# Ternary feed-forward stage: the convolution's middle tap from PE to DVE, the product with the token scales from DVE to GpSimd

## The reference, cut to what matters

```python
def act_quant(x):
    scale = 127.0 / jnp.clip(jnp.max(jnp.abs(x), axis=-1, keepdims=True), 1e-05)
    return jnp.clip(jnp.round(x * scale), -128, 127) / scale
def weight_quant(w):
    scale = 1.0 / jnp.clip(jnp.mean(jnp.abs(w)), 1e-05)
    return jnp.clip(jnp.round(w * scale), -1, 1) / scale
...
h = bit_linear(x, w1)                     # 256 -> 1024, both sides quantised
h = depthwise_conv1d(h.transpose(0, 2, 1), conv_w, conv_b)   # 3 taps along the tokens
h = jax.nn.silu(h.transpose(0, 2, 1))
return bit_linear(h, w2)                  # 1024 -> 256
```

## Time and profile before

| what | value |
|---|---|
| three timed runs | 4100.06, 4102.44, 4113.78 us (median 4102.44) |
| profiled execution | 4103.83 us, of which 4102.1 us is the span of the program |
| busy in the whole span | PE 3478.7 us (85%), DVE 2519.5 us (61%), ACT 1758.5 us (43%), POOL 1149.7 us (28%) |
| the changed stage | from about 736 to 1038 us of the span |
| POOL in this stage, 720 to 1040 us | 12.40 us busy |

### The profile page before, as it was taken

How to read it: one execution, slowest core, us unless ns; L and a number is a source line. 1 busy time by engine, 2 the same in 40 slices (tenths; PEclk the granted TensorE clock), 3 DMA queues, 4 the chain that set the end, 5 groups by cost and what they waited for, 6 DMA issues and landing times. The chain is left out here.

```text
span 4102.1 us, 68551 instructions
## 1 busy us (share of the span) xinstructions
PE 3478.7 (85%) x18821; PEld 1736.5 (42%) x18821; DVE 2519.5 (61%) x7412; ACT 1758.5 (43%) x2506; POOL 1149.7 (28%) x1242
## 2 busy tenths in 40 slices
PE   5999999799599999996997887887379999995797
PEld 2343343344233333334663555555223334335565
DVE  4666665677587777775215666677856666644531
ACT  1554545444044444452114666666525545550111
POOL 3343431000644444411113332231232221101132
PEclk8999999999699999997998989999679999995898
DMA  5322330000433223201008888898031122103142
GB/s 138 80 61 66 81 73 17 21 1 1 112 89 96 81 78 86 75 22 48 0 15 251 282 262 265 283 302 286 2 96 38 38 53 58 32 1 114 53 107 67
DMA packets 212161, 393.08 MB, mean 96 GB/s; under 512 B 24633, under 2 KB 76985, under 8 KB 211657
## 3 DMA queue, kind: packets, MB, share of 16 engines
q1 hardware_dynamic: 168777, 296.38, 26.2%
q10 hardware_dynamic: 36864, 83.90, 5.4%
q0 software_dynamic: 6144, 8.39, 1.2%
HBM read 189.88 MB, written 96.47 MB: 70 GB/s over the span
## 5 line engine op out<-in xcount | busy, mean ns | idle before, releaser
L428 DVE CUSTOM_DVE_ANT_0 A_sums<-A_p_ps,A_bias 128x512 bf16<-128x512 f32 x1536 | 1007.0, 687 | 418.1 <-PE A_p_ps L274 396.2
L501 ACT ACTIVATE A_probs<-A_p_ps 128x1024 f32<-128x1024 f32 x640 | 654.4, 1024 | 608.2 <-PE A_p_ps L293 595.9
L274 PE MATMUL A_p_ps<-A_k_stack,A_q_stack 96*128 96x512 bf16 x1536 | 514.2, 391 | 101.5 <-DVE A_nmax L428 91.5
L288 PE MATMUL A_p_ps<-A_q_stack,A_k_stack 99*128 99x512 bf16 x1536 | 461.3, 381 | 0.1
L303 PE MATMUL A_oT_ps<-A_probs,A_v_aug 128*17 128x512 f32 x3072 | 406.0, 600 | 3.2 <-ACT A_probs L501 2.4
L274 PEld LDWEIGHTS A_p_ps<-A_k_stack,A_q_stack 96*128 96x128 bf16 x1536 | 135.8, 98 | 485.4 <-DVE A_nmax L428 383.8
L293 PE MATMUL A_p_ps<-A_biasT,ident_bf 128*128 128x512 bf16 x1024 | 306.9, 380 | 0.0
L1000 PE MATMUL A_t_ps<-ident,A_scores 128*128 128x128 f32 x1280 | 206.8, 296 | 113.3 <-DVE A_probsT L1082 99.6
L1092 DVE CUSTOM_DVE_ANT_0 A_scores<-A_qk_ps,A_rel_in 128x384 f32<-128x384 f32 (+3 forms) x512 | 231.6, 485 | 78.7 <-PE A_qk_ps L977 76.0
L1082 DVE COPY A_probsT<-A_t_ps 128x1024 f32<-128x1024 f32 (+3 forms) x256 | 210.5, 822 | 107.8 <-PE A_t_ps L1000 100.0
L501 ACT ACTIVATE A_probs<-A_probs 128x1024 f32<-128x1024 f32 x128 | 135.3, 1057 | 312.7 <-DVE A_probs L443 312.7
(11 more groups left out here) (356 smaller groups left out, 5829.8 us busy)
## 6 DMA issues: line engine op xcount, KB each, us to landing
A_k_stack<-A_parts SPq DMA_DIRECT2D x192, 256.0 KB, 5.3
A_q_stack<-A_parts SPq DMA_DIRECT2D x192, 256.0 KB, 5.5
A_rel_dram<-A_rel_out ACTq DMA_DIRECT2D x64, 512.0 KB, 5.0
A_rel_in<-A_rel_dram SPq DMA_DIRECT2D x64, 512.0 KB
A_rel_dram<-A_rel_out ACTq DMA_DIRECT2D x64, 384.0 KB, 4.3
A_rel_in<-A_rel_dram SPq DMA_DIRECT2D x64, 384.0 KB, 4.8
A_ctxT<-in_ctxT SPq DMA_DIRECT2D x32, 512.0 KB, 6.2
A_mask_in<-in_mask SPq DMA_DIRECT2D x64, 256.0 KB, 4.1
```

The lines of the kernel that those rows point to most:

```text
L274: nc.tensor.matmul(p1_ps[i % 2][:, :], q_stack[0:KS, a_par, j * GH + i, t * P:(t + 1) * P], k_stack[0:KS, a_par, j * GH + i, :], start=Tru ...
L288: last = nc.tensor.matmul(p2_ps[half][:, i % 2, :], k_stack[:, par, j * GH + i, kb * P:(kb + 1) * P], q_stack[:, par, j * GH + i, :], star ...
L428: nc.vector.tensor_tensor_reduce(out=sums[:, i % NX, :], in0=p1_ps[i % 2][:, :], in1=bias[:, t, :], scale=-1.0, scalar=3.4028235e38, op0=A ...
L501: nc.scalar.activation(dst, src, ACT.Exp).then_inc(exp_done, 1)
```

## The change

- `tap_diag` keeps two blocks a unit (taps 0 and 2), and ACT builds 16 of them, not 24. `convolve` issues two fp32 matmuls, on `hs` shifted by 0 and by 2.
- The middle tap is a new DVE instruction, `add_centre`: `hs` times the tap (one scalar for each partition) plus `cv_ps`, written to a new SBUF tile `act_in` (`summed`). It waits for the unit's convolution and stands behind `round_unit` and ahead of `fold`. `silu` waits for `summed` and reads `act_in`. `cv_ps` and `hs` come free with `summed`.
- `quantise` moves from DVE to POOL and keeps its order by slots. On POOL, `inv_std(b+1)` stands in slot 1 ahead of that slot's `quantise`. `round_unit` stays on DVE and waits for POOL's product.

```diff
-        tap_diag = sb("tap_diag", [P, HC, 3, P], F32)
+        tap_diag = sb("tap_diag", [P, HC, 2, P], F32)
+        act_in = sb("act_in", [P, 2, S], F32)
...
+            def quantise(b, par, c):
+                if c == 0:
+                    pool.wait_ge(sc_ready, b + 1).then_inc(apart_pool, 1)
+                nc.gpsimd.tensor_tensor(act_out[:, par, c, :], act_out[:, par, c, :], sc_bc[:, par, :], ALU.mult).then_inc(u_done, 1)
+
+            def frame(b, par, slots):
+                for c in slots:
+                    if c == 1 and exists(b + 1) and exists(b):
+                        inv_std(b + 1)
+                    bq, pq, cq = quantised(b, par, c, LAG)
+                    if exists(bq):
+                        quantise(bq, pq, cq)
+
+            inv_std(0)
+            frames(pool, frame)
...
-                    pe.wait_ge(silu_done, unit(b, c) - 1)
-                for k in range(3):
-                    last = nc.tensor.matmul(cv_ps[c % 2][:, :], tap_diag[:, c, k, :], hs[:, c % 2, k:k + S],
-                                            start=k == 0, stop=k == 2)
+                    pe.wait_ge(summed, unit(b, c) - 1)
+                for k in range(2):
+                    last = nc.tensor.matmul(cv_ps[c % 2][:, :], tap_diag[:, c, k, :], hs[:, c % 2, 2 * k:2 * k + S],
+                                            start=k == 0, stop=k == 1)
...
-                    dve.wait_ge(conv_done, unit(b, c) - 1)
+                    dve.wait_ge(summed, unit(b, c) - 1)
...
+            def add_centre(b, c):
+                dve.wait_ge(conv_done, unit(b, c) + 1).then_inc(apart_dve, 1)
+                if not isinstance(b, int) or unit(b, c) >= 2:
+                    dve.wait_ge(silu_done, unit(b, c) - 1)
+                nc.vector.scalar_tensor_tensor(act_in[:, c % 2, :], hs[:, c % 2, 1:S + 1], taps[:, c, 1:2],
+                                               cv_ps[c % 2][:, :], op0=ALU.mult, op1=ALU.add).then_inc(summed, 1)
...
-                    if exists(bq):
-                        quantise(bq, pq, cq)
                     if exists(after[0]) and (c == HC - 1 or exists(b)):
                         scale(*after)
                     if exists(bq):
                         round_unit(bq, pq, cq)
+                    if exists(b):
+                        add_centre(b, c)
...
-                act.wait_ge(conv_done, unit(b, c) + 1).then_inc(apart_act, 1)
-                nc.scalar.activation(act_out[:, par, c, :], cv_ps[c % 2][:, :], ACT.Silu, bias=conv_bias[:, c:c + 1]).then_inc(silu_done, 1)
+                act.wait_ge(summed, unit(b, c) + 1).then_inc(apart_act, 1)
+                nc.scalar.activation(act_out[:, par, c, :], act_in[:, c % 2, :], ACT.Silu, bias=conv_bias[:, c:c + 1]).then_inc(silu_done, 1)
```

More of the change, by code:

```diff
@@ L1426, in ffn_bitnet @@
         h_done, h_scaled, conv_done, silu_done, folded = (sem(n) for n in ("h_done", "h_scaled", "conv_done", "silu_done", "folded"))
-        size_done = sem("size_done")
+        size_done, summed = sem("size_done"), sem("summed")
         peak_turned, sc_step, sc2_ready, diag2_ready = (sem(n) for n in ("peak_turned", "sc_step", "sc2_ready", "diag2_ready"))
@@ L1451, in _, with frames @@
             sp.dma_start(w2_in[:, :, :], w2T.rearrange("(c p) n -> p c n", p=P)).then_inc(w2_here, 16)
+        def frames(engine, frame):
+            frame(-1, 1, range(HC))
+            frame(0, 0, range(HC))
+            frame(1, 1, range(HC))
+            with engine.Fori(0, (B - 4) // 2) as twice:
+                for k in range(2):
+                    frame(twice * 2 + 2 + k, k, range(HC))
+            frame(B - 2, 0, range(HC))
+            frame(B - 1, 1, range(HC))
+            frame(B, 0, range(HC))
+            frame(B + 1, 1, range(LAG + 2))
         @block.gpsimd
@@ L1628, in batch_scales, with fold @@
                 nc.vector.tensor_scalar(inv2[:, par, :], amax2[:, :], mean_w[:, 1:2], None, ALU.mult).then_inc(sc2_ready, 1)
[L1630 to L1633, removed]
+            def fold(b, par, c):
+                dve.wait_ge(size_done, unit(b, c) + 1).then_inc(apart_dve, 1)
+                if c:
+                    dve.wait_ge(folded, unit(b, c))
+                nc.vector.tensor_tensor(peak[:, par, :], sizes[:, c % 2, :],
+                                        peak[:, par, :] if c else sizes[:, 0, :], ALU.max).then_inc(folded, 1)
             def round_unit(b, par, c):
@@ L1686, in frame @@
                         round_unit(bq, pq, cq)
+                    if isinstance(b, int) and b == 0 and c == 0:
+                        dve.wait_ge(taps_scaled, 1)
+                    if exists(b):
+                        add_centre(b, c)
                     before = (b, par, c - 1) if c else (b - 1, 1 - par, HC - 1)
@@ L1743, in _ @@
             for c in range(HC):
-                for k in range(3):
-                    last = nc.scalar.activation(tap_diag[:, c, k, :], ident[:, :], ACT.Copy, scale=taps[:, c, k:k + 1])
+                for k in range(2):
+                    last = nc.scalar.activation(tap_diag[:, c, k, :], ident[:, :], ACT.Copy, scale=taps[:, c, 2 * k:2 * k + 1])
             last.then_inc(tap_diags, 1)
```

## The result

The changed kernel takes 4157.69 us (median of four runs, 4154.24 to 4162.97) against 4101.25 us for the kernel before on the same chips: ratio 1.0124, 95% interval 1.0106 to 1.0141. It is slower by 56 us; 37 had been forecast, and 4157.69 lies in the upper part of the forecast's 4118 to 4164. The profiled run took 4162.97 us with a span of 4161.2 us, the slowest of the four.

The account below looks back on a forecast made before the run. PE bounds the kernel before; after it, DVE waits behind convolutions: 35.4 + 1.8 contention + 3.8 clock = 41.0 us a frame against 34.0, +35 for five frames, +1.6 for the rest, giving 4139 us. Range 4118 to 4164, at 0.66.

Parts of the forecast that it names:

- The bound and the relief: PE sets the pace now; it loses 6.9 us a frame, to 23.7, and DVE's 26.2 stands above it.
- Part A: Frame from add_centre(0) to add_centre(3): 14.5 us, with a 2.5 us stall in slot 1 and PE waiting about 4.
- The second segment: Frame from PE's scales to add_centre(3): forecast at 5.6 us, against 4.61 before.
- Part B: Frame from add_centre(3) to add_centre(5): 9.85 us, PE's wait before contract growing from 2.15 to about 4.5.
- Part C: Frame from add_centre(5) to the next frame's add_centre(0): 10.7 us without contention.
- the loop's turn: Turn of the loop, once: adds what it adds now, 0.4 us a frame in the mean.
- POOL against DVE: DVE's fold and round_unit held beside POOL's products: 1.8 us a frame, bounds nothing and about 5.
- The clock: PE's clock falls after two gaps of 4 us, 1.9 us each: 3.8 us a frame, bounds nothing and 6.
- The rest of the stage: Outside the five frames: opening -2.4 us, frame 0 +0.5, frames 1 and 7 +1.5, tail +2; sum +1.6.
- the order alone: Rival: clock holds and POOL fits between DVE's instructions; +7 us, 4109; chance 0.13.
- the permanently low clock: Rival: PE stays at 1.2 GHz between two long waits; +15 us a frame, 4179; chance 0.08.
- the faster one: Rival: no slot 1 stall, both contention terms under 1; -5 us a frame, 4076; chance 0.09.

Follow-up runs that it names:

- e6: Changed kernel with DVE's extras except batch_scales moved ahead of round_unit and add_centre: ratio 1.0026 to the kernel before, 37.6 us a frame.
- e10: Changed kernel, most DVE extras ahead of add_centre, out_rows heading slot 4, batch_scales ahead of fold, POOL's inv_std behind slot 1's product: ratio 1.0009, 34.6 us a frame.
- e9: Kernel before the change with only out_rows moved from the end of its DVE slot to its head: ratio 0.9980, 32.0 us a frame.
- e3: Changed kernel with POOL's two inverse-deviation instructions behind slot 1's product, not ahead of it: 4146.89 us, ratio 1.0081 to the kernel before.
- e4b: Changed kernel with POOL's product replaced by a fill of a scratch tile that reads nothing: ratio 1.0082 to the kernel before, 41.4 us a frame.
- e5: Changed kernel with idle transposes filling PE's two gaps, ahead of scales and of slot 4's first contraction: ratio 1.0113 to the kernel before, 41.5 us a frame.
- e11: Kernel before with the product on POOL, out_rows at the head of its slot, inv_std behind slot 1's product: ratio 1.0038, 37.1 us a frame.
- e2: Kernel before with only the product moved to POOL, PE keeping three taps: ratio 1.0066, 40.3 us a frame.

## Why the prediction was right, and where its sum was off

**The bound and the relief.** Right. PE lost its 6.9 us a frame and the frame grew. What had been beside the convolution came behind it, as the walk through the queues said; e6 and e10 show that it was the order for the most part, since they change nothing else. Against e9, which has the row update moved too, 2.6 us a frame are left that order did not give back.

**Part A.** 14.5 plus its contention and clock terms made 17.0; measured 17.6. The stall in slot 1 (2.34 us of idle time; "about 2.5") and PE's wait (4.7 to 5.5; "about 4") are there, and e3 shows the stall on the path. The second segment was forecast at 5.6 and came out at 5.65 in three frames, which is luck: it was set there by POOL's first product and the rounding held behind it (held 0.7 to 0.95 us there, put at 0.25), a path that the sum didn't have. In frames 3 and 4 it was 7.0, since the fall of the clock, put at 1.9, slowed everything in it.

**Part B.** 9.85 plus 1.25 plus 1.9 made 13.0; measured 13.6. PE's wait before the contraction was put at 4.5 and is 6.2 to 6.9. The contention term came out at its size by other instructions: one fold held for 0.3 us where two for 0.5 and a rounding for 0.25 had been counted, and 1.05 for the small `row_scales` op, which the sum had missed. It has one input of four columns and spans 1.22 us beside a product where it takes 0.17.

**Part C.** The largest miss in a term: 11.1 against 12.4. Without the loop's turn the part is 11.5, not 10.7. In frame 4 PE, done with convolution 7, waits 0.69 us for ACT to copy the next batch's turned rows (L1747) before it can project them; the sum had no ACT in this chain. The loop's turn adds 4.15 us in frame 3, where I had carried over 2: DVE's idle time there is put down to nothing that the profile shows (913.52), and PE passes after it run at the low clock. Why the turn costs more than before stays open.

**POOL against DVE.** The mechanism was right, the size was low: 1.8 a frame forecast, while the four held instructions of frame 4 are (1.25 - 0.41) + (1.09 - 0.41) + (0.98 - 0.68) + (1.22 - 0.17) = 2.9 us. Taking the reads away (e4b) gave 2.1 back, with shorter POOL instructions and the roundings still held.

**The clock.** Mechanism right, size high in the mean: 3.8 forecast; keeping PE busy gave 2.1. In frame 5 of e5, the only one in which the clock held at both places, the two segments together are 8.32 us, where the same frame of the changed kernel has 10.05 and the mean of the five is 11.09. In three frames of five the first fall is nearly hidden behind the held rounding.

**The rest of the stage.** +1.6 forecast, 55.04 - 47.77 = +7.3 measured, the largest miss beside the frames: the opening up to the first silu gave 2.9 back (2.4 forecast), but frame 0 took 4.0 more, not 0.5. The weights' rounding took its 3.7 us behind `add_centre(0)` as forecast, the first statistics stood behind it, and PE then idled 4.6 us and ran its next passes slowly, which the sum left out; frame 1 at +2.9 and frame 7 at +2.0, together 1.5 forecast; the tail at +1.2, for 2. How much of the 4.1 us by which all other stages differ belongs to the change isn't known; no edit touches them, and whole runs of the kernel before spread over more (4092.6 to 4114.7 us in one set).

**Sum.** 7.0 us a frame were forecast, 9.5 came. The terms off were part C with the loop's turn (+1.3), part A's end (+0.6) and part B (+0.5). With the +5.7 of the rest they make the 18 us by which the stage passed the forecast; all are on the same side, and the range was wide enough to hold them. Of the rivals, the order alone was too small a case (its held instructions and clock falls are there), the permanently low clock didn't come (0.85 in the mean), and the faster one failed at the point given for it: the stall and both contention terms were there.

## What to carry to other kernels

When an engine takes over work that waits for another engine's result of the same slot, everything behind it in its queue moves from beside that engine to behind it: look first at who waits for the instructions that stand there, and move them ahead of the new wait. A product moved to POOL isn't free for DVE: each rounding, small op or two-operand op beside it may be held to its end, and the place to check is whether PE waits for something queued behind those. Whether the move pays depended on the order here: it cost 4.7 us a frame in one and gave 1.6 in another. Before taking work off the engine that sets the pace, look at its longest wait: one call moved in the old kernel gave 9.7 us in the stage, while the whole change, which takes a third of the convolution's passes off PE, cost 55.

## What the runs showed that I had not expected

- A DVE `tensor_scalar` of four columns is held like wide ones: 1.22 us for 0.17. The reduction over 1024 columns next to it never was (1204 to 1205 ns in the six that lie beside a product), nor was the row update, which reads PSUM and SBUF (468 to 472 ns).
- A fill on POOL, which reads nothing, held roundings (up to 1208 ns) and no two-operand fold (at most 686 ns in the eight beside a fill).
- POOL's product itself stretches where DVE gets in between: 41 of 64 take 1252 to 1274 ns, and the nine that start while a fold is under way take 1712 to 1722. One fold that started 0.1 us ahead of its product took 690 ns, and the product 1717.
- The same six passes behind PE's gap took 4.43 us after 3.30 us of idling in e11 and after 2.14 us in the kernel before, and 4.87, with the contraction ahead of them slow too (1.01 us for 0.60), after 4.76 us in e2. Behind the other gap of 2.17 us the clock had not fallen: the length of the gap alone doesn't tell.
